# Attention normalisers: adding and inverting them four heads at a time on GpSimd instead of a reciprocal on VectorE

## The reference

```
q = quantise(layernorm(x) @ Wq + bq, /4)      # 16 heads of 16
k, v = quantise(ctx @ Wkv + bkv)              # 2048 keys
attn = softmax(q @ k.T)                       # 2048 x 2048 per head
attn = round(attn / (max(attn) / 255)) * (max(attn) / 255)
x = x + tanh(g) * ((attn @ v) @ Wp + bp)
```

## Time and profile before

| | us |
|---|---|
| median of 3 runs | 1159.33 (1158.93 to 1160.88) |
| the profiled execution | 1159.07 |
| its span | 1157.4 |
| VectorE busy | 947.1 |
| ScalarE busy | 888.7 |
| TensorE matmul busy | 1059.9 |
| GpSimd busy | 699.3 |
| reduction for the maximum, L425 | 610.1 |
| exponentials, L485 | 609.8 |
| casts, L537 | 479.2 |

### The profile page before, as it was taken

How to read it: one execution, slowest core, us unless ns; L and a number is a source line. 1 busy time by engine, 2 the same in 40 slices (tenths; PEclk the granted TensorE clock), 3 DMA queues, 4 the chain that set the end, 5 groups by cost and what they waited for, 6 DMA issues and landing times.

```text
span 1157.4 us, 24150 instructions
## 1 busy us (share of the span) xinstructions
PE 1059.9 (92%) x8396; PEld 603.4 (52%) x8396; DVE 947.1 (82%) x1734; ACT 888.7 (77%) x1544; POOL 699.3 (60%) x625
## 2 busy tenths in 40 slices
PE   7988898889988988998898988999999999999997
PEld 4743444444444444444444446756654465557775
DVE  6999999999999999999999996963327788943335
ACT  4679999999999999999999997645543576834441
POOL 3016888888788887878788778247761000653432
PEclk9999999999999999999999999999999999999999
DMA  6798898887888888988875765847938002523336
GB/s 195 119 168 147 170 171 161 174 174 161 170 176 168 166 163 172 169 158 175 174 116 106 119 110 92 256 136 213 325 111 328 1 1 48 178 87 108 98 97 235
DMA packets 388799, 176.36 MB, mean 152 GB/s; under 512 B 330413, under 2 KB 373650, under 8 KB 388680
## 3 DMA queue, kind: packets, MB, share of 16 engines
q1 hardware_dynamic: 381976, 157.85, 62.6%
q0 software_dynamic: 6480, 16.77, 4.3%
q10 hardware_dynamic: 224, 0.20, 0.1%
HBM read 52.70 MB, written 43.59 MB: 83 GB/s over the span
## 4 chain that ended last, share of the span: by engine, by line
PE 50%; DVE 33%; ACT 5%; issue 5%; DMA 3%; POOL 2%; SPq 1%; POOLq 0%; ACTq 0%; DVEq 0%
DVE top L425 27%; PE bank L234 10%; PE bank L220 9%; PE bank L252 4%; PE bank L2634 4%; PE bank L1598 3%; PE bank L1199 3%; PE bank L2650 3%; PE bank L1186 2%; PE bank L1175 2%; ACT weight L485 2%; PE bank L1871 1%; PE bank L1616 1%; PE bank L682 1%; POOL dispatched_rows L1841 1%
## 5 line engine op out<-in xcount | busy, mean ns | idle before, releaser
L485 ACT ACTIVATE weight<-bank,bias,sq_all 128x1024 uint8<-128x1024 f32 x512 | 609.8, 1201 | 19.1 <-PE bank L234 13.8
L425 DVE TENSOR_REDUCE top<-bank 128x1 f32<-128x512 f32 (+1 forms) x683 | 610.1, 951 | 11.6 <-PE bank L220 1.1
L537 POOL CAST weight<-turned 128x2048 bf16<-128x2048 uint8 x256 | 479.2, 1892 | 36.6 <-DMA turned<-weight 16.1
L234 PE MATMUL bank<-kT,query 128*128 128x512 bf16 x1024 | 307.7, 382 | 12.5 <-ACT weight L485 5.3
L252 PEld LDWEIGHTS bank<-v_sb,weight 128*128 128x128 bf16 x4096 | 172.2, 97 | 103.4 <-POOL weight L537 1.3
L220 PE MATMUL bank<-kT,qspace 64*128 64x512 bf16 x687 | 135.0, 387 | 54.9 <-DVE top L425 54.9
L252 PE MATMUL bank<-v_sb,weight 128*128 128x16 bf16 x4096 | 172.5, 169 | 1.0 <-POOL weight L537 1.0
L220 PE MATMUL bank<-kT,query 128*128 128x512 bf16 x337 | 127.8, 379 | 1.6 <-DVE top L425 1.4
L234 PEld LDWEIGHTS bank<-kT,query 128*128 128x128 bf16 x1024 | 59.7, 96 | 104.4 <-ACT weight L485 62.6
L1841 POOL DMA_INDIRECT dispatched_rows<-qspace,put x32 | 37.1, 1160 | 116.1 <-DVE qspace L2391 106.9
L485 ACT ACTIVATION_READ_ACCUMULATOR weight<-bank,bias,sq_all 128x1 f32 x512 | 101.7, 199 | 0.0
(11 more groups left out here) (351 smaller groups left out, 1458.0 us busy)
## 6 DMA issues: line engine op xcount, KB each, us to landing
dispatched_rows<-zeros SPq DMA_DIRECT2D x32, 524.0 KB, 3.2
answered_rows<-zeros SPq DMA_DIRECT2D x16, 512.0 KB, 3.4
late<-answered_rows SPq DMA_DIRECT2D x16, 512.0 KB, 6.3
erow<-dispatched_rows SPq DMA_DIRECT2D x39, 131.0 KB
wgu<-in_L_ffn_w_gate SPq DMA_DIRECT2D x26, 176.0 KB, 3.3
wgu<-in_L_ffn_w_up SPq DMA_DIRECT2D x26, 176.0 KB, 3.4
query<-qspace SPq DMA_DIRECT2D x32, 128.0 KB, 3.1
turned<-weight SPq DMA_TRANSPOSE x256, 3.1
```

Of the source, the lines that this page charges most:

```text
L234: mm = pe.matmul(unit[u % 2][:, v * 512:(v + 1) * 512], query2[:, t % 2, h, :], kT[:, h // 2, first + v * 512:first + (v + 1) * 512], star ...
L425: ve.tensor_reduce(top[:, first:first + count], bank[:, first % 3:first % 3 + count, :], AX.X, ALU.max).then_inc(s_max, 1)
L485: ac.activation(weight8[:, n % BYTES, u * 1024:(u + 1) * 1024], unit[u], ACT.Exp, bias=bias[:, n:n + 1], scale=sq_all[:, n:n + 1], accum_o ...
L537: po.tensor_copy(weight[:, n % 3, :, :, :].rearrange("p c q two -> p (c q two)"), turned8[:, n % 3, :, :].rearrange("p c q -> p (c q)").bi ...
```

## The change

GpSimd no longer adds the sums of a whole tile behind its last head. At each n % 4 = 1 from n = 5 on, behind the cast of head n, it adds the partial sums of heads n - 5 to n - 2 (128x4) and raises the result to the power of minus one, by an elementwise power with a tile that holds -1.0. So the last four heads of tile t (16t+12 to 16t+15) are done at n = 16t + 17. The last group follows the loop. VectorE's reciprocal and its semaphore go; the product waits for the tile's four inversions. The waits of ScalarE and GpSimd on tile t - 2 count in the new steps.

```
+            inverse = sa("inverse", [P, 4])
...
             def finish_tile(ve, t):
-                ve.wait_ge(s_rn, t + 1)
-                ve.reciprocal(rnorm[:, t % 2, :], rnorm[:, t % 2, :]).then_inc(s_rnv, 1)
-                ve.wait_ge(s_rnv, t + 1)
+                ve.wait_ge(s_rn, H // 4 * (t + 1))
                 ve.wait_ge(s_val, H * (t + 1))
...
                     if h == 0 and t >= 2:
-                        ac.wait_ge(s_rn, t - 1)
+                        ac.wait_ge(s_rn, H // 4 * (t - 1))
...
+                def invert_normalisers(n):
+                    t, h = divmod(n, H)
+                    if h == 0 and t >= 2:
+                        po.wait_ge(s_ofree, t - 1)
+                    part = rnorm[:, t % 2, h:h + 4]
+                    po.wait_ge(s_exp, 2 * (n + 4))
+                    po.tensor_tensor(part, norm[:, t % 2, h:h + 4, 0], norm[:, t % 2, h:h + 4, 1], ALU.add).then_inc(s_sums, 1)
+                    po.wait_ge(s_sums, n // 4 + 1)
+                    po.tensor_tensor(part, part, inverse[:], ALU.pow).then_inc(s_rn, 1)
...
-                    t, h = divmod(n, H)
-                    if h == H - 1:
-                        if t >= 2:
-                            po.wait_ge(s_ofree, t - 1)
-                        po.wait_ge(s_exp, 2 * (n + 1))
-                        po.tensor_tensor(rnorm[:, t % 2, :], norm[:, t % 2, :, 0], norm[:, t % 2, :, 1], ALU.add).then_inc(s_rn, 1)
+                    if n % 4 == 1 and n > 4:
+                        invert_normalisers(n - 5)
+                invert_normalisers(NHEAD - 4)
...
+                    step(po.memset(inverse[:], -1.0))
```

More of the change, by code:

```diff
@@ L177, in program @@
             s_wide, s_val = sem("weights_widened"), sem("head_values_summed")
-            s_ofree, s_rn, s_rnv = sem("tile_outputs_taken"), sem("normalisers_added"), sem("normalisers_inverted")
+            s_ofree, s_sums, s_rn = sem("tile_outputs_taken"), sem("normalisers_added"), sem("normalisers_inverted")
             s_q2 = [sem(f"padded_queries_copied_{k}") for k in range(2)]
```

## The result

The changed kernel takes 1184.18 us (1180.94 to 1184.71 over 5 runs) against 1159.33: ratio 1.0206, 95% interval 1.0192 to 1.0219. It is 24.9 us slower. Slower was forecast, and 1184.18 lies in the stated range (1158.5 to 1190), though above the forecast's own range (1162 to 1183); the predicted loss was 9.9 us against the median, less than half of the real one. A tile lasts 40.86 us ((669.75 - 138.54) / 13, from product to product) where about 40.0 was forecast. The profiled execution is the shortest of the five, 1180.94, or 21.9 above the profiled one of before.

The account below looks back on a forecast made before the run. VectorE was taken to bound the attention heads. 1159.07 - 4.2 (reciprocals removed) + 13.0 (product stalls) + 1.3 (GpSimd's load) = 1169.2 us, range 1158.5 to 1190, the forecast's own 1162 to 1183.

Parts of the forecast that it names:

- What bounds the kernel, and what the reciprocals are worth: Attention heads: VectorE's work sets a tile's length; removing 15 reciprocals of 0.28 us from its path gains 4.2 us.
- The moved release, D + p + 0.15: Tile ends: VectorE's product is released this long after the old reciprocal's start; stalls of 13.0 us together.
- D: End of cast 16t+17 less the old reciprocal's start: mean +0.77 us in tiles 0 to 3, -0.26 in tiles 4 to 14.
- more in tiles 0 to 3: Sign that the forecast is right: the tile period grows from 39.39 to about 40.0 us, more in these tiles than later.
- the price p: Duration of GpSimd's 128x4 power, shown by no row: 0.7 us taken, the middle between rows of 0.22 and 1.21.
- GpSimd's own load: Each four heads gain p + 0.37 = 1.07 us on GpSimd; 0.34 short in four early tiles, +1.3 us.
- The rival in which GpSimd is the bound throughout: Past p = 1.55 (0.9 in early tiles) GpSimd's work sets the pace; at p = 2 about 1200 us; chance 0.15.
- Absorption: Rival: VectorE's 10.1 us of gaps in the heads close, stalls shrink to some 4, time stays at 1159 us; chance 0.10.

Follow-up runs that it names:

- e3: The kernel before without VectorE's reciprocals and their semaphore, the product multiplying by the sums (inverse left out): 1155.39 us, ratio 0.9957.
- e4: The kernel before plus 63 adds and powers on GpSimd at the changed kernel's places, written to an unread spare tile: 1164.53 us, ratio 1.0040.
- e7: The kernel before with a VectorE maximum over 1400 elements ahead of the product of tiles 0 to 14, holding it 1.61 us each: 1187.59 us, ratio 1.0241.
- e11: The kernel before with a VectorE maximum over 500 elements ahead of the product of tiles 0 to 14, holding it 0.67 us each: 1172.66 us, ratio 1.0092.
- e12: The kernel before with a VectorE maximum over 2800 elements ahead of the product of tiles 0 to 14, holding it 3.07 us each: 1234.52 us, ratio 1.0630.
- e1: The changed kernel with each inversion one cast earlier, behind the cast of head n at n % 4 = 0: 1160.26 us, ratio to the kernel before 1.0000.
- e5: e1 with GpSimd's 16 bias additions spread to every third group of four heads: 1157.16 us, ratio to the kernel before 0.9969.

## Why the prediction was wrong in size

- **What bounds the kernel, and what the reciprocals are worth:** right. VectorE's work set the pace before; 4.2 us predicted, 4.2 in the trace of e3.
- **The moved release, D + p + 0.15:** right as a mechanism. With the real p of 1.035 the same D give 4 x (0.77 + 1.185) + 11 x (-0.26 + 1.185) = 18.0 us; the waits are 17.2, or 18.5 counted with the records' overlap of 15 x 0.08. The "more in tiles 0 to 3" holds as well (1.90 us each against 0.87). Nor is the total luck: for tiles 0, 2, 4, 8 and 13 it gives 1.75, 2.16, 1.26, 0.47 and 1.07, and the waits with 0.08 added are 1.64, 1.88, 1.28, 0.66 and 1.01.
- **The failed term: the price p.** "The middle, 0.7" was a guess between a row that is no power and another that is none; it was 1.035. That is 15 x 0.335 = 5.0 us of stalls. The Trainium skill (GPSIMD Engine Reference, Engine selection) sends elementwise add, multiplication and maximum to VectorE; for a reciprocal, which it doesn't name there, the traces here point the same way: for one tile 0.24 us on VectorE against 64 / 16 x 1.034 = 4.1 on GpSimd.
- **GpSimd's own load:** 1.3 predicted. By the same formula the real p gives p + 0.37 = 1.405 in four heads, 0.67 over the wait, or 4 x 0.67 = 2.7; it was 2.2 in the changed kernel and 3.9 by itself (e4). Right in place and kind, too small by the same p. The rival in which GpSimd is the bound throughout did not occur: it still waits 27.5 us for VectorE. But p passed the 0.9 that this rival set for the early tiles, and it is mostly in tiles 0 to 3 that the load costs time.
- **A term that was missing: TensorE's clock.** I wrote that nothing makes up for the stall, and stopped there; TensorE's stand has a price of its own, 4.6 us in the profiled execution. The sum with the measured p is 1159.07 - 4.2 + 18.0 + 2.7 = 1175.6, with the clock 1180.2, against 1180.94. So of the 11.7 us by which the profiled execution lies above the forecast 1169.2, the price p makes 6.4 and the clock 4.6. The other four executions have mean clocks of 0.987 to 0.990 in place of 0.991 and lie 2.5 to 3.8 us higher; by e7's slope the clock is 0.8 to 3.2 of that. Only their times and clocks are on record, so the rest stays open.
- **Absorption** is refuted by e7: the gaps of 10.1 us take up nothing.

## What to carry to other kernels

Moving work off the bound engine pays only if its result is still in time: write down where the receiver stands today and where the new result will land, because a step that leaves the bound engine can cost it more as a wait than it did as work. Measure an operation without a row in some idle stretch before building on it. And where work fills another engine's slack, its largest piece between two waits and what shares that group can count more than the average.

## What the runs showed of the hardware

- A power on GpSimd takes 1.035 us for 4 columns of 128 partitions, 1.667 for 8 and 2.91 for 16 (once 3.6): some 0.4 us and 0.156 per column. A multiplication of 4 columns takes 0.20.
- TensorE's granted clock fell from full to 0.50 (1.2 in place of 2.4 GHz) for 3.4 or 6.8 us. In the 5 us before each fall in the heads TensorE's longest stand was 0.6 to 3.3 us (e11: 0.60, e12: 3.26). Behind 15 holds of VectorE there were 2 falls at 0.67 us, 4 at 1.61 and 15 at 3.07, the last nearly all of double length. A stretch of 3.4 us cost VectorE about 1 us of gaps. Equal holds did and did not bring one; what decides was not found, and it differs from one execution to the next, which goes with a wider spread: 11 us over the four executions of e7, 3 us over those of the kernel before beside it. Holds aren't the only occasion: e1, e3 and e5, in which no product waits, have a fall of 3.4 or 6.8 us at 738.9, 733.3 and 734.6, behind the heads, after TensorE stood for 0.7. The kernel before runs at 0.50 only in its last 4.7 us, which makes its mean 0.998.
